# Attention outputs normalised between two block transpositions on VectorE

## What is computed

```python
x = x + 0.5 * moe(layernorm(x))      # 32 experts of 96, top 8, sum of kept weights to 0.8
x = x + attention(layernorm(x))      # 16 query heads, 4 key/value heads, 16 wide, rope
x = x + 0.5 * moe(layernorm(x))
# attention, per head:
scores = einsum('bhqd,bhkd->bhqk', q, k) * 16 ** -0.5
out = einsum('bhqk,bhkd->bhqd', softmax(scores), v)
return einsum('bsh,oh->bso', out, Wo)
```

## Time and profile before

| | |
|---|---|
| median of 3 runs | 2287.29 us (2285.87 to 2287.63) |
| profiled execution, its time | 2285.59 us |
| its span | 2283.8 us |
| TensorE busy | 2212.3 us, 97% |
| VectorE busy | 1577.6 us, 69% |
| ScalarE, GpSimd busy | 1187.6 us and 1063.1 us |
| mean granted TensorE clock | 1.000 |

### The profile page before, as it was taken

The page is one execution under the profiler, slowest core; times in us unless marked ns, Lnnn a source line. Parts: engine busy times, 40 slices in busy tenths (PEclk is TensorE's granted clock), DMA queues, the critical chain, the costliest instruction groups (busy, mean ns, idle before and its releaser), DMA issues.

```text
span 2283.8 us, 47219 instructions
## 1 busy us (share of the span) xinstructions
PE 2212.3 (97%) x18832; PEld 1472.5 (64%) x18832; DVE 1577.6 (69%) x3138; ACT 1187.6 (52%) x1917; POOL 1063.1 (47%) x864
## 2 busy tenths in 40 slices
PE   2999999999999999999999999999999999999998
PEld 2888875555555565555555565555555655688887
DVE  7766679887777877877877876777777753455543
ACT  4433331556656656565566566566656656533332
POOL 1766653443443443443434434333433434465655
PEclk9999999999999999999999999999999999999999
DMA  5211121011111120111211111110110110011110
GB/s 216 81 43 34 39 57 31 21 43 31 31 45 41 34 60 24 32 39 34 49 44 40 28 38 36 25 42 16 36 42 11 37 33 20 15 49 38 26 39 20
DMA packets 176389, 92.45 MB, mean 40 GB/s; under 512 B 122020, under 2 KB 168356, under 8 KB 175400
## 3 DMA queue, kind: packets, MB, share of 16 engines
q1 hardware_dynamic: 176024, 89.39, 15.1%
q10 hardware_dynamic: 144, 0.03, 0.0%
HBM read 62.87 MB, written 11.80 MB: 33 GB/s over the span
## 4 chain that ended last, share of the span: by engine, by line
PE 89%; DVE 7%; issue 1%; POOL 1%; ACT 0%; DMA 0%; POOLq 0%; DVEq 0%; ACTq 0%
PE PS L1200 42%; PE PS L1218 21%; PE PS L1230 11%; PE PS L1263 11%; DVE arena L975 2%; PE PS L1242 1%; PE PS L1182 1%; PE PS L1299 1%; PE PS L1290 1%; DVE XN L855 1%; DVE turned L938 0%; DVE arena L952 0%; DVE arena L937 0%; DVE arena L960 0%; POOL arena L608 0%
## 5 line engine op out<-in xcount | busy, mean ns | idle before, releaser
L1200 PE MATMUL PS<-XT,WGU 128*128 128x256 f16 x9216 | 1114.1, 273 | 37.8 <-DVE WGU L821 20.8
L1200 PEld LDWEIGHTS PS<-XT,WGU 128*128 128x128 f16 x9216 | 876.4, 98 | 266.5 <-issue 136.6
L613 POOL TENSOR_TENSOR arena<-arena 128x512 f16<-128x512 f32 x384 | 450.1, 1172 | 1109.4 <-ACT arena L693 1109.2
L975 DVE TENSOR_REDUCE arena<-PS 128x1 f32<-128x512 f32 x1024 | 657.5, 683 | 322.4 <-PE PS L1230 319.9
L716 ACT ACTIVATE arena<-PS,fac 128x512 f32<-128x512 f32 x1024 | 646.4, 684 | 243.4 <-PE PS L1242 242.3
L686 ACT ACTIVATE arena<-PS,fac 128x512 f32<-128x512 f32 x384 | 263.8, 687 | 773.1 <-PE PS L1200 773.1
L1218 PE MATMUL PS<-WD,arena 128*128 128x256 f16 x4608 | 568.2, 273 | 7.3 <-DVE X L967 4.7
L1218 PEld LDWEIGHTS PS<-WD,arena 128*128 128x128 f16 x4608 | 430.6, 98 | 153.4 <-issue 94.9
L608 POOL TENSOR_TENSOR arena<-arena 128x512 f32<-128x512 f32 x384 | 501.1, 1305 | 46.4 <-DVE arena L960 37.7
L952 DVE SCALAR_TENSOR_TENSOR arena<-arena,PS 128x512 f32<-128x512 f32 x384 | 260.9, 679 | 263.1 <-ACT arena L686 262.2
L1230 PE MATMUL PS<-arena 48*128 48x512 f16 x1024 | 312.6, 382 | 3.3 <-DVE arena L975 2.4
(11 more groups left out here) (113 smaller groups left out, 690.8 us busy)
## 6 DMA issues: line engine op xcount, KB each, us to landing
arena<-ce_scratch SPq DMA_DIRECT2D x256, 128.0 KB, 3.3
arena<-wgu SPq DMA_DIRECT2D x4, 1536.0 KB, 12.9
arena<-q_scratch SPq DMA_DIRECT2D x192, 32.0 KB
arena<-ktab_c SPq DMA_DIRECT2D x16, 256.0 KB, 4.1
q_scratch<-arena SPq DMA_DIRECT2D x32, 128.0 KB, 1.8
out<-X SPq DMA_DIRECT2D x8, 512.0 KB, 2.9
X<-wd SPq DMA_DIRECT2D x2, 1536.0 KB, 22.8
X<-x SPq DMA_DIRECT2D x1, 3072.0 KB, 11.9
```

The costliest lines, as they stand in the source:

```text
L613: pool.tensor_tensor(hs[1][:, d % HS, :], tw[d % 2], hs[0][:, d % HS, :], ALU.subtract).then_inc(lo_done, 1)
L975: dve.tensor_reduce(mx[:, half * REP * QT + c:half * REP * QT + c + 1], PS[:, B_MAX + half, :], AX_X, ALU.max).then_inc(max_taken, 1)
L1200: ins = pe.matmul(PS[:, b, j * HALF_G:(j + 1) * HALF_G], WGU[w][:, kt, part * CHUNKS + c + j, :], XT[r][:, k % 2, kt, half * HALF_G:(half ...
```

## The change

`oT`, `otok`, the high and low parts and the copies of the bank go. VectorE transposes the bank in blocks of 32x32 straight out of PSUM (`turn_outputs`, at the visit that ends the half unit): then the queries stand on the partitions and each block of 32 columns holds a head's 16 outputs and its sum. `normalise` divides in place in the next slot (reciprocal of 16, product of 256 columns). `outputs_split` on GpSimd now runs once per half unit on 256 columns and puts high and low side by side in `opair`, 32 to a block; `turn_back`, two slots later, transposes blocks of 32x32 again, 512 fp16 columns, into `ocol`. So on the partitions high and low alternate by 16, for four heads; the output weights are laid out twice in the same way. The projection sums over both and has 2 by 2 matmuls for each 128 tokens instead of 3: 8 an event. It includes low by low, which was left out before. The events "out_T" vanish, and "out_y" stands 3 to 6 slots behind a fourth half unit. RING goes from 3 to 4.

```diff
-RING = 3
+RING = 4
...
-    done = 0
-    for hv in range(2 * UNITS):
-        d = place(max(done, SLOT_OF[quad_visit(8 * hv + 7)] + 1), ("out_T", hv, 0))
-        done = d
-        if hv % 4 == 3:
-            d += 5
-            for j in range(4):
-                d = place(d + 1, ("out_y", hv // 4, j))
+    for v in range(UNITS // 2):
+        d = OUT_AT[4 * v + 3] + 2
+        for j in range(4):
+            d = place(d + 1, ("out_y", v, j))
...
+OUT_AT = [SLOT_OF[quad_visit(QT * hv + QT - 1)] + 1 for hv in range(2 * UNITS)]
...
-        WO = [sb(f"WO{h}", [P, KT, HID], F16) for h in range(2)]
+        WO = [sb(f"WO{h}", [P, KV, HID], F16) for h in range(2)]
...
-        n_small = [KT * EXPERTS, KT * QB * P, KT * K_ROWS, KT * KV * HD, KT * HID]
+        n_small = [KT * EXPERTS, KT * QB * P, KT * K_ROWS, KT * KV * HD, KV * HID]
...
+            def outputs_split(hv):
+
+                pool.wait_ge(o_norm, hv + 1)
+                if hv:
+                    pool.wait_ge(o_cols, hv)
+                pool.tensor_copy(opair[:, :, 0, :], orow[:, :, 0:HD]).then_inc(o_hi, 1)
+                pool.wait_ge(o_hi, hv + 1)
+                pool.tensor_tensor(opair[:, :, 1, :], orow[:, :, 0:HD], opair[:, :, 0, :], ALU.subtract).then_inc(o_lo, 1)
...
-                q = quad_at(v)
-                if q is not None and q % QT == QT - 1:
-                    hv = q // QT
-                    act.wait_ge(pv_done, q + 1)
-                    if hv:
-                        act.wait_ge(o_T, hv)
-                    act.activation(oT, PS[:, B_O, :], ACT.Copy).then_inc(o_sb, 1)
...
             def visit(v):
-                f = v + AHEAD
+                f, q = v + AHEAD, quad_at(v)
...
+                if q is not None and q % QT == QT - 1:
+                    turn_outputs(q // QT)
+
+            def turn_outputs(hv):
+
+                dve.wait_ge(pv_done, QT * (hv + 1))
+                if hv:
+                    dve.wait_ge(o_lo, hv)
+                dve.transpose(orow_f, PS[:, B_O, :]).then_inc(o_rows, 1)
+
+            def normalise(hv):
+
+                dve.wait_ge(o_rows, hv + 1)
+                link(dve.reciprocal(rd, orow[:, :, HD]))
+                dve.tensor_tensor(orow[:, :, 0:HD], orow[:, :, 0:HD], rd.unsqueeze(2).to_broadcast([P, 512 // 32, HD]),
+                                  ALU.mult).then_inc(o_norm, 1)
+
+            def turn_back(hv):
...
+                dve.wait_ge(o_lo, hv + 1)
...
+                dve.transpose(ocol[:, u % 2, half * 512:half * 512 + 512], opair_f).then_inc(o_cols, 1)
...
+                if d in OUT_AT:
+                    normalise(OUT_AT.index(d))
+                if d - 2 in OUT_AT:
+                    turn_back(OUT_AT.index(d - 2))
...
-                        pe.wait_ge(o_sb, q // QT)
+                        pe.wait_ge(o_rows, q // QT)
...
-                for h in range(2):
-                    pe.wait_ge(o_cols[h], 64 * (v + 1))
+                pe.wait_ge(o_cols, 4 * (v + 1))
                 for i in range(2):
                     t = 2 * j + i
-                    for m, (w, r) in enumerate(PASSES):
-                        ins = pe.matmul(PS[:, bank, i * HID:(i + 1) * HID],
-                                        ocol[r][:, t * P:(t + 1) * P], WO[w][:, v % 2, :],
-                                        start=(m == 0), stop=(m == 2))
+                    for a in range(2):
+                        for w in range(2):
+                            ins = pe.matmul(PS[:, bank, i * HID:(i + 1) * HID], ocol[:, a, t * P:(t + 1) * P],
+                                            WO[w][:, v % 2 * 2 + a, :], start=(a == 0 and w == 0), stop=(a == 1 and w == 1))
```

More of the change, by code:

```diff
@@ L249, in build @@
         F_TANH, F_Y, F_LOGIT, F_EXP, F_O, F_T = (fac[:, i:i + 1] for i in range(6))
-        ARENA = 19616
+        ARENA = 18832
         arena = sb("arena", [P, ARENA])
@@ L355, in build @@
         rows_T, rows_out = sem("rows_T"), sem("rows_out")
-        o_sb, o_T, o_norm, o_hi, o_lo, yo_done, xo_done = (
-            sem("o_sb"), sem("o_T"), sem("o_norm"), sem("o_hi"), sem("o_lo"), sem("yo_done"), sem("xo_done"))
-        o_cols = [sem(f"o_cols{h}") for h in range(2)]
+        o_rows, o_norm, o_hi, o_lo, o_cols, yo_done, xo_done = (
+            sem("o_rows"), sem("o_norm"), sem("o_hi"), sem("o_lo"), sem("o_cols"), sem("yo_done"), sem("xo_done"))
         stored = sem("stored")
@@ L651, in _ @@
                         rows_low(norm_of_group(k + 1))
[L652 to L655, removed]
+                if d in OUT_AT:
+                    outputs_split(OUT_AT.index(d))
         @block.scalar
@@ L1032, in event @@
                     join(n, j, bank)
-                if name == "out_T":
-                    normalise(n, bank)
                 if name == "out_y":
@@ L1284, in visit @@
                         score_exp(v // FILLS, v % FILLS * 2 + half)
-            def transpose_outputs(hv, bank):
-                pe.wait_ge(o_sb, hv + 1)
-                for t in range(4):
-                    ins = pe.transpose(PS[:, bank, t * P:(t + 1) * P], oT[:, t * P:(t + 1) * P], identf[:, :])
-                ins.then_inc(o_T, 1)
             def project_outputs(v, j, bank):
-                for h in range(2):
-                    pe.wait_ge(o_cols[h], 64 * (v + 1))
+                pe.wait_ge(o_cols, 4 * (v + 1))
                 for i in range(2):
                     t = 2 * j + i
-                    for m, (w, r) in enumerate(PASSES):
-                        ins = pe.matmul(PS[:, bank, i * HID:(i + 1) * HID],
-                                        ocol[r][:, t * P:(t + 1) * P], WO[w][:, v % 2, :],
-                                        start=(m == 0), stop=(m == 2))
+                    for a in range(2):
+                        for w in range(2):
+                            ins = pe.matmul(PS[:, bank, i * HID:(i + 1) * HID], ocol[:, a, t * P:(t + 1) * P],
+                                            WO[w][:, v % 2 * 2 + a, :], start=(a == 0 and w == 0), stop=(a == 1 and w == 1))
                 ins.then_inc(yo_done, 1)
@@ L1332, in event @@
                     taken[bank] = (j_taken, JOINS * n + j + 1)
-                if name == "out_T":
-                    transpose_outputs(n, bank)
-                    taken[bank] = (o_norm, n + 1)
                 if name == "out_y":
@@ L1396, in layouts @@
         "wv": on_partitions(a["L0_attn_Wv"]),
-        "wo": on_partitions(a["L0_attn_Wo"]),
+        "wo": np.ascontiguousarray(np.repeat(a["L0_attn_Wo"].T.reshape(KV, REP, 1, HD, HID), 2, axis=2)
+                                   .transpose(1, 2, 3, 0, 4).reshape(P, -1)),
     }
```

43 lines of the change are left out of this document (8 added, 35 removed).

## The result

| | before | after |
|---|---|---|
| median | 2287.29 us | 2277.91 us |
| all runs | 2285.87 to 2287.82 (7) | 2277.55 to 2281.35 (7) |
| ratio, 95% interval | | 0.9963 [0.9953, 0.9973] |
| profiled execution | 2285.59 us | 2277.70 us |
| its span | 2283.8 us | 2275.9 us |

The change makes the kernel 0.37% faster, 9.4 us by the medians. That is more than the 0.2% that a measurement can tell from nothing, and the forecast of 2283.9 was 6 us too high, and the range given for 8 in 10, from 2278.5, is missed by 0.6 us. The time is that of the first rival, the whole net of TensorE. The two profiled executions differ by 7.9 us, and it is these 7.9 us that can be followed instruction by instruction; where the other 1.5 lie is told under the hardware at the end.

The account below looks back on a forecast made before the run. TensorE, busy 97% of the span, was taken to set the time almost alone; -14.7 + 7.0 + 2.8 + 1.0 + 0.5 = -3.4 us gave 2282.2 profiled, 2283.9 as median with 1.7 added; 8-in-10 range 2278.5 to 2289.

Parts of the forecast that it names:

- the first rival: Whole kernel: VectorE's idle absorbs all and moved adds save up to 3 us; -7 to -10 us, 2277 to 2280; chance 0.40.
- Removed from TensorE: 32 blocks of four fp32 transposes go from TensorE, each worth its start-to-start distance: -14.7 us.
- Added to TensorE: The 32 output projections have 8 matmuls instead of 6, 64 more at 0.109 us each: +7.0 us.
- Four exponential buffers: ScalarE's wait for a free exponential buffer never ends last with three, so a fourth gains nothing.
- The turned bank: TensorE's next values must wait for `turn_outputs` on the output bank; it fits with 1.5 us to spare: nothing.
- Setup: Output weights of 1024 columns: larger load adds nothing, maximum is absorbed, low part's split costs more: +0.5 us.
- Moved: Projections three slots earlier: some adds get free of routing, others land in it; counted at 0, within -3 and +3.
- What of it TensorE meets: Of 64 VectorE insertions in the attention stretch, 13 touch TensorE's next use of a bank: +2.8 us, 0 to about 8.
- headway lost: About five removed transpositions precede TensorE waits for a join or routing, which only lengthen: +1.0 us, 0 to 2.
- VectorE becomes the bound: More than a quarter of VectorE's 46 us of transpositions reaches TensorE; kernel slower by over 0.2%; chance 0.09.

Follow-up runs that it names:

- e5: Kernel before with every block of four fp32 transposes on TensorE issued twice: median 2299.53 us against 2286.04, ratio 1.0059.
- e9: Kernel after with 6 matmuls a projection instead of 8, part of the low weights' product left out: median 2273.17 us, 0.9941 of the kernel before.
- e3: Kernel after with three exponential buffers instead of four, the memory of four kept: median 2279.20 us, 0.9967 of the kernel before.
- e1: Kernel after with the projections three slots later, as far behind the last half unit as before: median 2283.84 us, 0.9983 of the kernel before.
- e12: Kernel after with the normalisation's multiply on GpSimd and the output weights' low part split in slot 20: median 2278.28 us, 0.9958 of the kernel before.
- e7: Kernel after with the normalisation and the transposition back last in their slots on VectorE: median 2277.06 us, 0.9961 of the kernel before.
- e10: Kernel after with only the second VectorE transposition, `turn_back`, done twice: median 2286.85 us, 0.9999 of the kernel before.
- e6: Kernel after with both VectorE transpositions done twice: median 2293.57 us, 1.0032 of the kernel before.
- e2: Kernel before with two more VectorE reductions of 512 columns per half unit, at the places of the two transpositions: median 2288.15 us, ratio 1.0006.
- e8: Kernel after with VectorE's part of a join ahead of the norm piece and the normalisation: median 2281.44 us, 0.9978 of the kernel before.

## Why the prediction went wrong

**Right.** *Removed from TensorE* (-14.7 us): exact, and the doubling (e5) shows that a further 14.0 us of blocks cost 13.5. *Added to TensorE* (+7.0): 6.9, and e9 takes the same 7.0 off the distances. *Four exponential buffers* (nothing): e3. *The turned bank* (nothing): TensorE has no wait for `turn_outputs` in any kernel. *Setup* (+0.5): the split took 2.17 us where it had 1.64, and TensorE's wait went from 0.16 to 0.69 us. What that part had wrong is that the larger load adds nothing and the maximum over it is absorbed: VectorE waits 0.4 us for the output weights to land and then reduces for 2.83 us instead of 2.29 ahead of the layer norm, so TensorE's first transposition starts at 15.2 us instead of 13.95. The first gate starts 0.6 us later. The durations of the two transpositions (0.72 and 0.71 us) measured 0.706 and 0.697. The weight loads' wait was to be 55 to 70 us in the stretch and is 64.5.

**The step that failed** is *Moved*, "I count it at 0, within -3 and +3". It is worth -4.1 us, and outside its own bounds; 2.9 of it are the waits for adds, 3.1 us before and 0.2 after, and the rest stood ahead of blocks that went or moved. The rows for it were there: 3.1 us of waits behind the add, and another 0.9 us ahead of the transposes and the projections themselves. What was weighed against them, adds now standing "in slots 19, 20 and 18 of a group, where the routing is", did not come: the whole wait for adds after is 0.2 us. Counting slot by slot where the new adds stand and what lies ahead of them on VectorE would have given it; instead two unlike things were set off against each other. e1 shows the cause by itself: the same work three slots later costs 4.6 us in the kernel after.

**Mis-sized.** *What of it TensorE meets* (+2.8) and *headway lost* (+1.0) together came to 2.9 us: the join's 1.5 and 1.4 elsewhere. The placement was poor, though. The wait of 2.03 us at 1120 us was not foreseen; it stood at 0.30 before. There the norm's pieces, the normalisation and the join are in one slot; the multiply used to read PSUM and took 0.42 us, and from SBUF it took 1.67. The prediction's 0.25 us for each held multiply gave 8 us in all, and 6.95 were measured (15 of 32 held), so the sum was right and its spread mattered: 1.25 us in one place stand ahead of a wait that grew by 1.5 (how much of it is the hold is not shown by itself, since e12 and e7 hand it on), and most of the other 14 cost nothing that shows. The Trainium skill (SBUF — State Buffer, Who interferes with whom) says that not only an operation with two SBUF inputs but also a scalar operation of that engine in a two-port mode blocks against GpSimd for a whole instruction. The trace of e12 fits, with the four norm pieces at 1.65, 0.71, 0.53 and 0.83 us beside 0.40 free, and so does that of the kernel before, with one at 0.84; that half of the rule was not used in the prediction.

**By the sum:** -14.7 + 6.9 - 4.1 + 2.9 + 0.5 + 0.6 = -7.9, against -3.4 forecast. Of the 4.5 us between them 4.1 are the moved adds, 0.9 the insertions and headway and 0.1 the matmuls; the later start takes 0.6 back. The last 1.5 us up to the medians' 9.4 came from the reference: the prediction set the median of before 1.7 us above its profiled execution and carried that over, while the kernel after's median lies 0.2 above its own.

**The rivals.** *The whole net of TensorE arrives* (0.40) had the time right and half of the reason: it asked that VectorE's idle absorb all, and VectorE took 2.9 us, which the adds paid for. *VectorE becomes the bound* (0.09) is nearer than its chance made it look: with 22 us more on VectorE (e10) the kernel is no faster than before by the medians, with 45 more (e6) it is slower. The Trainium skill (VectorE: DVE Perf Modes, Rules for kernel authors) advises TensorE for transposing 128x128. Here, where TensorE sets the time, leaving that way paid: 14.7 us of TensorE were bought with 45 us of VectorE at a price of 2.9, and of 6.9 more matmul time.

**Open.** Whether the 0.6 us at the first gate belong to the change: it starts at 41.7, 42.3 and 42.9 us in the three executions with the setup of before (before, e2, e5) and at 42.1 to 43.4 in the eleven with that of after, so one pair does not tell. That the clock falls described at the end lie behind the last 1.5 us is read from runs, not forced by an experiment.

## What to carry to other kernels

Where TensorE is busy 97% of the time, a step taken from it is worth the distance from its start to the next block's, and a step moved within its order can be worth more than one removed when it stands behind VectorE's longest pieces (up to 1.1 us at a place here, against 0.46 for a block): list for every slot what lies ahead of each operation that frees a PSUM bank, before and after. Work given to the second engine is nearly free until it reaches TensorE's next use of a bank, and then cost 0.3 us or more for each us here; measure how far that edge is by doubling the new work once. An operation moved from PSUM to SBUF operands can be held by GpSimd, and the hold moved on to the next such operation when this one was taken away.

## What the runs showed of the hardware

**A wait of 2 us can cost more than 2 us.** In some executions TensorE's granted clock fell to the lower of its two levels, 1.2 GHz, for 3.4 us, right behind a wait of TensorE of 1.9 to 3.0 us. This is the kernel with six matmuls, from the join at 1120 us (the wait ahead of it is 2.03 us, as in the kernel after):

```profile
1120.00:1121.00 1.00, 1.00 (x7) 0.73 (x6) 1.00 (x3) 0.45 (x1) 0.74 (x1) 0.56 0.83 250
1121.00:1122.00 1.00, 1.00 (x7) 0.59 (x4) 1.00 (x3) 0.00 (x0) 0.00 (x0) 0.50 0.26 51
1122.00:1123.00 1.00, 1.00 (x6) 0.13 (x4) 0.84 (x2) 0.00 (x1) 0.00 (x0) 0.50 0.00 0
1123.00:1124.00 1.00, 1.00 (x8) 0.66 (x7) 1.00 (x3) 1.00 (x2) 0.81 (x1) 0.74 0.00 0
```

The third number from the end is the granted clock: 0.56, 0.50, 0.50, 0.74, and 1.00 after. TensorE has 6 to 8 matmuls in a us there; the kernel after, in the execution shown, has the same wait and no fall:

```profile
1120.00:1121.00 1.00, 0.97 (x9) 0.90 (x10) 1.00 (x2) 0.63 (x1) 0.93 (x1) 1.00 0.86 273
1121.00:1122.00 1.00, 0.90 (x9) 0.38 (x6) 1.00 (x3) 0.05 (x1) 0.00 (x0) 1.00 0.48 123
```

The clock missing from these four rows adds up to 0.44 + 0.5 + 0.5 + 0.26 = 1.7 us. What a fall cost in block starts was 1.3 us at 1120 (e3, e10), 1.5 to 1.7 at 209, 1.6 at 1292, and 0.4 to 0.7 at 53. The falls came at few places: at about 53, 209 (behind a wait of 2.33 us for X) and 1120 us, in this execution or that, and once each at 312 (e8, behind a wait for X that had grown to 3.0) and 1292 us (e10, behind a join's wait of 1.9, 1.2 in the kernel after). The profiled executions of before and after have none inside, that of e9 two (209 and 1120), that of e10 four. Of the seven runs of the kernel after, the four with a mean clock of 1.000 took 2277.6 to 2277.9 us, and the three with 0.999 took 2279.1, 2279.5 and 2281.4. So in this kernel the scatter is of such steps. The seven of before lie in two groups as well, 2285.9 to 2286.0 and 2287.3 to 2287.8, with the median in the upper; after's median is in the lower, and that is how 7.9 us in the traces become 9.4 by the medians. That before's groups are also a fall apart is likely but not shown: in its later runs beside the experiments the mean clock does not sort the times so well (2285.3 to 2287.1 us at 1.000, 2285.1 to 2289.2 at 0.999).

**A hold is one instruction of the other engine long.** The multiply with two SBUF inputs takes 424 ns free and up to 2101; the longest started 0.3 us into a GpSimd operation of 2.12 us and ended 0.3 us behind it. Before, the same product with one input from PSUM took 424 ns in the mean, so it was never held. The split of the output weights in slot 8 was held too, in both kernels: 1.64 us before for 512 columns, where that of WQ takes 0.74, and 2.17 after for 1024, where it takes 1.28 in slot 20. There it starts first, and GpSimd's operation of 1.27 us takes 2.25.

**The low part of the weights** costs 1.04 ns a column here: free, 0.74 us for 512 columns and 1.28 for 1024; the 0.9 us of hold is the same in both kernels, so the change adds 0.53.
